# Attention products on four quarters of TensorE's array, roots with two dependent steps, and a reordered instruction schedule, in a convolution, attention and expert kernel

## What is computed

```python
# x: (32, 64, 32, 32)
x = x + conv(groupnorm(x))          # relu/sigmoid maps, their outer product (16x16), a 1x1 conv
t = tokens(x)                       # (32, 1024, 64)
# attention, on y = layernorm(t); H = 8 heads of D = 8
q, k, v = y @ Wq, y @ Wk, y @ Wv
Q, K = elu(q) + 1, elu(k) + 1
KV  = einsum('nshd,nshv->nhdv', K, v)
Z   = 1 / (einsum('nlhd,nhd->nlh', Q, K.sum(axis=1)) + eps)
msg = layernorm(einsum('nlhd,nhdv,nlh->nlhv', Q, KV, Z) @ Wm)
t = t + y + layernorm(relu(concat([y, msg]) @ W1) @ W2)
# experts, on z = layernorm(t)
t = t + sum_e cw[e] * (gelu(z @ W1[e] + b1[e]) @ W2[e] + b2[e])
```

## Time and profile before

| what | value |
|---|---|
| median of 3 runs | 1252.85 us (1252.80 to 1252.86) |
| profiled execution | 1252.97 us, its span 1251.2 us |
| PE busy | 1092.2 us, 87% of the span |
| DVE busy | 852.6 us, 68% |
| ACT busy | 699.9 us, 56% |
| POOL busy | 362.2 us, 29% |
| granted TensorE clock, mean | 0.978 of full speed |

### The profile page before, as it was taken

How to read it: one execution, slowest core, us unless ns; L and a number is a source line. 1 busy time by engine, 2 the same in 40 slices (tenths; PEclk the granted TensorE clock), 3 DMA queues, 4 the chain that set the end, 5 groups by cost and what they waited for, 6 DMA issues and landing times.

```text
span 1251.2 us, 14277 instructions
## 1 busy us (share of the span) xinstructions
PE 1092.2 (87%) x5238; PEld 501.4 (40%) x5238; DVE 852.6 (68%) x1751; ACT 699.9 (56%) x960; POOL 362.2 (29%) x276
## 2 busy tenths in 40 slices
PE   4776598979899799988989899997989979999897
PEld 2454244423544244442454334542444424534232
DVE  5656766697658876488585876669665887646433
ACT  3443365664665645755646656556466565566454
POOL 0100031233313423134313333124331333313466
PEclk8888699999999999999999999999999999999999
DMA  2110392008610094003920058100861019300570
GB/s 103 34 34 1 75 202 63 1 18 180 145 34 18 21 219 108 11 18 78 215 65 1 18 125 199 34 1 17 183 142 34 18 32 220 73 1 18 124 167 34
DMA packets 15797, 96.39 MB, mean 77 GB/s; under 512 B 2992, under 2 KB 5104, under 8 KB 11504
## 3 DMA queue, kind: packets, MB, share of 16 engines
q1 hardware_dynamic: 15728, 95.49, 32.7%
HBM read 77.66 MB, written 9.44 MB: 70 GB/s over the span
## 4 chain that ended last, share of the span: by engine, by line
PE 58%; DVE 25%; ACT 12%; issue 4%; DMA 1%; POOL 0%; DVEq 0%; POOLq 0%; SPq 0%; ACTq 0%
PE HP L647 10%; PE HP L662 9%; PE R L518 7%; PE R L586 5%; PE R L477 4%; PE R L488 4%; PE R L470 4%; DVE T L983 3%; PE R L532 3%; DVE TM L1100 2%; ACT H L788 2%; DVE SM L956 2%; PE R L561 2%; PE R L593 2%; PE R L662 2%
## 5 line engine op out<-in xcount | busy, mean ns | idle before, releaser
L828 POOL TENSOR_TENSOR XB<-TM,XB 128x512 f32<-128x512 f32 x256 | 324.8, 1289 | 825.2 <-DVE TM L1100 825.2
L788 ACT ACTIVATE H<-HP,W 128x1024 f32<-128x1024 f32 x224 | 237.7, 1114 | 98.9 <-PE HP L647 97.8
L647 PE MATMUL HP<-XF,W1E 64*128 64x512 f32 x1024 | 256.8, 620 | 25.5 <-DVE TM L1100 24.6
L662 PE MATMUL HP<-H,W 128*64 128x512 f32 x896 | 226.2, 611 | 29.1 <-ACT H L788 29.1
L1100 DVE SCALAR_TENSOR_TENSOR TM<-HP,B2S,CWB 128x512 f32<-128x512 f32 x224 | 159.4, 742 | 105.7 <-PE HP L662 102.1
L647 PEld LDWEIGHTS HP<-XF,W1E 64*128 64x128 f32 x1024 | 87.8, 186 | 150.4 <-DVE TM L1100 79.3
L956 DVE TENSOR_REDUCE SM<-T 128x8 f32<-128x512 f32 x128 | 86.3, 685 | 50.7 <-ACT T L725 49.3
L662 PEld LDWEIGHTS HP<-H,W 128*64 128x64 f32 x896 | 49.0, 135 | 176.9 <-ACT H L788 133.8
L725 ACT ACTIVATE T<-R 128x512 f32<-128x512 f32 x128 | 74.7, 597 | 79.1 <-PE R L518 77.7
L932 DVE SCALAR_TENSOR_TENSOR BIG<-R,T 128x512 f32<-128x512 f32 x128 | 79.8, 683 | 33.7 <-PE R L470 33.3
L488 PE MATMUL R<-W,T 128*128 128x128 f32 x512 | 78.0, 296 | 19.9 <-DVE T L975 19.0
(11 more groups left out here) (117 smaller groups left out, 1417.8 us busy)
## 6 DMA issues: line engine op xcount, KB each, us to landing
CWB<-gates_hbm SPq DMA_DIRECT2D x32, 1536.0 KB, 20.4
CWB<-gates_hbm SPq DMA_DIRECT2D x32, 512.0 KB, 6.7
X<-x SPq DMA_DIRECT2D x16, 512.0 KB, 6.5
BIG<-XN SPq DMA_DIRECT2D x32, 256.0 KB, 3.9
out<-XB SPq DMA_DIRECT2D x16, 512.0 KB, 2.7
W<-wpack SPq DMA_DIRECT2D x1, 1176.0 KB, 7.0
gates_hbm<-CWR SPq DMA_DIRECT2D x16, 64.0 KB, 1.6
W1E<-w1e SPq DMA_DIRECT2D x1, 512.0 KB, 8.4
```

Of the source, the lines that this page charges most:

```text
L647: last = mm(HP[u % BATCH][:, half(k)], W1E[img(k), e, :], XF[img(k), 1 - par, s, half(c)], start=True, stop=True)
L662: last = mm(sums_of(b, u)[img(k), :], w("w2e")[:, C * e:C * e + C], activated(b, u)[:, k, :], start=True, stop=True)
L788: f(activated(b, u).rearrange("p k t -> p (k t)"), HP[u % BATCH][:, :], ACT.Gelu, bias=col(B1E + e))\
L828: nc.gpsimd.tensor_tensor(acc, TM[:, u % BATCH, :], acc, ALU.add).then_inc(acc_done, 1)
```

## The change

It has three parts.

1. **Quarters.** `query` and `numerator` no longer use the block-diagonal 128x128 matrices but four products of 64x64 each, for a slot's two halves and two images. In the first half of the tokens image r goes from partitions `img(r)` to `img(r)`, in the second half it crosses to the other 64 partitions, so that the four products stand on four different quarters of the array; `numerator` crosses back. For the crossed half the key sums (`KS`), the values' matrix (`KVM`), the head mask (`HM2`) and `SPREAD` are needed in crossed form too. That adds a product with a swap matrix (`SWAP`) after each transpose of `kv_turn`, a second multiplication into `KS` on DVE, a copy of twice the width on ACT (`KXT`), a second product in `kv_values`, a multiplication of twice the width into `KVM`, and some small DMAs at the start. `query` now waits for both halves of `XB`, and `numerator` of slot 1 waits for L1006 before its first half, not its second.
2. **Roots.** `hz*y` is carried along as `hy`, so that a round has two steps that depend on each other, and an update of `hy` that is issued ahead of the update of `y` without a wait of its own.
3. **Schedule.** H and Y letters and some stages stand elsewhere in `SCHEDULE`. Entries that an engine has no part in leave its order alone. What differs on the engines: PE and ACT have one H ahead of `gates` and not behind it; `high_0`, `info_1` begin with slot 1; the order of `low_1` to `high_1` has its H after `low_1` and not between `info_1` and `low_1`; `first_unit` stands one batch earlier, so that 9 batches of a group run in its first turn and 7 in its second, where there were 8 and 8; an H that stood behind `hidden_1` stands ahead of `hidden_0`; `hidden_out` begins with slot 1 and its second slot comes ahead of the Y, and `tokens_3` begins with slot 0; `features_3.1` comes ahead of the Y.

The diff, cut to its core:

```diff
@@ SCHEDULE
-    ("channel_stats", ""), ("gates", "H"), ("gate_tokens", "Y"), ("gate_exp", ""), ("group_stats", "H"),
-    ("group_norm", "Y"), ("choose_1", ""), ("info_mask_0", "HY"), ("choose_2", "HY"), ("info_mask_1", "H"),
+    ("channel_stats", "H"), ("gates", ""), ("gate_tokens", "Y"), ("gate_exp", ""), ("group_stats", "H"),
+    ("group_norm", "Y"), ("choose_1", ""), ("info_mask_0", "HYH"), ("choose_2", "Y"), ("info_mask_1", "H"),
     ("gate_rows", "Y"), ("info_0.0", ""), ("info_0.1", "H"), ("low_0.0", ""), ("low_0.1", "Y"),
-    ("high_0.0", "H"), ("high_0.1", ""), ("info_1.0", "Y"), ("low_1.0", ""), ("info_1.1", "H"),
-    ("low_1.1", ""), ("high_1.0", ""), ("high_1.1", "Y"), ("first_unit", ""), ("conv_out.0", ""),
-    ("conv_out.1", ""), ("finish_1", ""), ("centre_1.0", ""), ("weights_1", ""), ("centre_1.1", ""),
-    ("rstd_1", "H"), ("norm_1.0", "Y"), ("features_1.0", ""), ("norm_1.1", "H"), ("features_1.1", ""),
+    ("high_0.1", ""), ("high_0.0", "H"), ("info_1.1", ""), ("info_1.0", "Y"), ("low_1.1", ""),
+    ("first_unit", ""), ("low_1.0", "H"), ("high_1.0", ""), ("high_1.1", "Y"), ("finish_1", ""),
+    ("conv_out.0", ""), ("conv_out.1", ""), ("centre_1.0", ""), ("centre_1.1", "H"), ("rstd_1", ""),
+    ("norm_1.0", ""), ("weights_1", "Y"), ("features_1.0", ""), ("norm_1.1", "H"), ("features_1.1", ""),
...
-    ("message.0", ""), ("message.1", ""), ("rstd_2", "H"), ("norm_2.0", ""), ("norm_2.1", "Y"),
-    ("features_2.0", ""), ("features_2.1", ""), ("hidden_0.0", ""), ("hidden_0.1", ""), ("hidden_1.0", ""),
-    ("hidden_1.1", "H"), ("hidden_out.0", "Y"), ("hidden_out.1", ""), ("tokens_3.1", ""),
-    ("tokens_3.0", "H"), ("rstd_3", "Y"), ("norm_3.0", "H"), ("norm_3.1", ""), ("features_3.0", "Y"),
-    ("features_3.1", ""), ("centre_4.0", ""), ("centre_4.1", ""), ("rstd_4", ""), ("finish_0", "H"),
-    ("norm_4.0", ""), ("norm_4.1", "Y"), ("features_4.0", ""), ("features_4.1", ""),
+    ("message.0", ""), ("message.1", ""), ("rstd_2", ""), ("norm_2.0", ""), ("norm_2.1", "HY"),
+    ("features_2.0", ""), ("features_2.1", "H"), ("hidden_0.0", ""), ("hidden_0.1", ""), ("hidden_1.0", ""),
+    ("hidden_1.1", ""), ("hidden_out.1", ""), ("hidden_out.0", "Y"), ("tokens_3.0", ""), ("tokens_3.1", ""),
+    ("rstd_3", "HY"), ("norm_3.0", ""), ("norm_3.1", "H"), ("features_3.0", ""), ("features_3.1", "Y"),
+    ("centre_4.0", ""), ("centre_4.1", "H"), ("rstd_4", ""), ("norm_4.0", ""), ("norm_4.1", "Y"),
+    ("features_4.0", ""), ("features_4.1", ""), ("finish_0", ""),
@@ PE
+        def crossed(c):
+            return [(r, r ^ c) for r in range(2)]
                 def query(slots):
-                    for s, c in pieces(slots):
-                        pe.wait_ge(xb_part[s], at(a + 1, c))
-                        mm(R[s][:, half(c)], w("wq"), XN[:, s, half(c)], start=True, stop=True).then_inc(qk_ps[s], 1)
+                    for s in slots:
+                        pe.wait_ge(xb_part[s], at(a + 1, LAST))
+                        for c in range(NCH):
+                            for r, k in crossed(c):
+                                last = mm(R[s][img(k), half(c)], w("wq", img(r))[:, img(r)], XN[img(r), s, half(c)],
+                                          start=True, stop=True)
+                            last.then_inc(qk_ps[s], 1)
                 def kv_turn(slots):
...
+                        nc.tensor.transpose(R[s][:, 0:P], KX[:, s, 0:P], w("ident")).then_inc(kvt_ps[s], 1)
+                        mm(R[s][:, CH:CH + 1], SWAP[:, :], KX[:, s, P:P + 1], start=True, stop=True).then_inc(ksum_ps[s], 1)
                 def kv_values(slots):
...
-                        mm(R[s][:, 0:P], KXT[:, s, :], w("wv"), start=True, stop=True).then_inc(kvm_ps[s], 1)
+                        for c in range(NCH):
+                            last = mm(R[s][:, P * c:P * c + P], KXT[:, s, C * c:C * c + P], w("wv"), start=True, stop=True)
+                        last.then_inc(kvm_ps[s], 1)
                 def numerator(slots):
-                    for s, c in pieces(slots):
-                        if c == 0:
-                            pe.wait_ge(kvm_done[s], a + 1)
-                        if (s, c) == (G - 1, LAST):
+                    for s in slots:
+                        pe.wait_ge(kvm_done[s], a + 1)
+                        if s == G - 1:
                             pe.wait_ge(den_eps, a + 1)
-                        mm(R[s][:, half(c)], KVM[:, s, :], Q[s][:, half(c)], start=True, stop=True).then_inc(num_ps[s], 1)
+                        for c in range(NCH):
+                            for r, k in crossed(c):
+                                last = mm(R[s][img(k), half(c)], KVM[img(r), s, c, img(k)], Q[s][img(r), half(c)],
+                                          start=True, stop=True)
+                            last.then_inc(num_ps[s], 1)
@@ ACT
                 def kv_turn(slots):
-                        f(KXT[:, s, :], R[s][:, 0:P], ACT.Copy).then_inc(kvt_done[s], 1)
+                        f(KXT[:, s, :].rearrange("p (n c) -> p n c", n=2), R[s][:, 0:P].unsqueeze(1).broadcast_to([P, 2, P]), ACT.Copy)\
+                            .then_inc(kvt_done[s], 1)
@@ DVE
                 def rsqrt(n, slots):
-                    hz, t, y = (SM[:, k, span, 0:n] for k in (1, 2, 3))
+                    hy, hz, t, y = (SM[:, k, span, 0:n] for k in range(4))
                     link(v.tensor_scalar(y.bitcast(I32), hz.bitcast(I32), -0.5, RSQRT_GUESS, ALU.mult, ALU.add))
-                    for _ in range(3):
-                        link(v.tensor_tensor(t, y, y, ALU.mult))
-                        link(v.tensor_tensor(t, t, hz, ALU.mult))
+                    link(v.tensor_tensor(hy, hz, y, ALU.mult))
+                    for last in (False, False, True):
+                        link(v.tensor_tensor(t, hy, y, ALU.mult))
+                        if not last:
+                            count(v.scalar_tensor_tensor(out=hy, in0=t, scalar=-1.5, in1=hy, op0=ALU.add, op1=ALU.mult))
                         link(v.scalar_tensor_tensor(out=y, in0=t, scalar=-1.5, in1=y, op0=ALU.add, op1=ALU.mult))
                 def key_value(slots):
-                        v.tensor_copy(KX[:, s, :], R[s][:, 0:P]).then_inc(kx_done[s], 1)
...
+                        v.tensor_copy(KX[:, s, :], R[s][:, 0:P + 1]).then_inc(kx_done[s], 1)
+                        key_sums(s, 0, R[s][:, P:P + 1])
+                def kv_turn(slots):
+                    for s in slots:
+                        dve.wait_ge(ksum_ps[s], a + 1)
+                        key_sums(s, 1, R[s][:, CH:CH + 1])
                 def kv_values(slots):
...
-                        v.tensor_tensor(KVM[:, s, :], R[s][:, 0:P], w("headmask"), ALU.mult).then_inc(kvm_done[s], 1)
+                        v.tensor_tensor(KVM[:, s, :, :].rearrange("p n c -> p (n c)"), R[s][:, 0:2 * P],
+                                        HM2[:, :], ALU.mult).then_inc(kvm_done[s], 1)
```

More of the change, by code:

```diff
@@ L380, in _ @@
                 sp.dma_start(GB[E * i:E * i + E, :], gb).then_inc(gb_in, 16)
+            masks = COLS["headmask"][0]
+            swaps = COLS["ident"][0]
+            sp.wait_ge(prep_done, 1)
+            for r, k in crossed(1):
+                sp.dma_start(HM2[img(r), P:2 * P], wpack[img(k), masks:masks + P]).then_inc(swap_in, 16)
+                sp.dma_start(SWAP[img(r), :], wpack[img(k), swaps:swaps + P]).then_inc(swap_in, 16)
             def parts(a, b, par):
```

47 lines of the change are left out of this document (30 added, 17 removed).

## The result

| | before | changed |
|---|---|---|
| median | 1252.86 us | 1232.61 us |
| runs | 1252.80 to 1254.65 (4) | 1229.98 to 1236.50 (4) |
| profiled execution, its span | 1252.97, 1251.2 us | 1232.37, 1230.6 us |
| ratio, 95% interval | | 0.9837, 0.9810 to 0.9865 |

The changed kernel is 1.6% faster.

The account below looks back on a forecast made before the run. PE was taken as close to the bound (132.15 of 146 us busy, 58% of the chain). Six steady turns at -3.0 us (-18), turn 0 -1.1, turn 1 +0.1, drain -4.75: -23.75 from 1252.97, so 1229 us; range 1221 to 1243.

Parts of the forecast that it names:

- Numerator: Numerator on the chain: one round per slot makes it 1.8 us shorter, 1.2 gained before reciprocal and combination limit it.
- Crossed copies: Extra swap products, wider copies and doubled products in kv_turn: cost of nothing to 0.9 us a turn, taken as 0.15.
- Roots: Each root from guess to scaling: 0.25 us saved, bounds nothing and 0.45; four in a turn, -1.0 us.
- (a): H ahead of gates, in the routing: with the group root's 0.25 us, 0.4 us sooner, bounds 0 and 0.6.
- (b): Outer product order: DVE's wait for PE at its end goes, -0.45 us a turn, bounds -0.9 and +0.5.
- (c): H ahead of hidden_0, in the hidden layer: about even, -0.1 us a turn, bounds -1 and +1.5.
- Turn 0: First turn: no Y between denominator and numerator, the reciprocal already bounds it, so only roots count: -1.1 us.
- rival of the clock: TensorE's clock falls in new idle places at query and numerator: 3 us a turn, 1250 us; chance 0.05.
- Turn 1: Second turn: gains 2.4 us, loses 2.5 (bounds 0 and 3.9) for one more batch; +0.1 us together.
- The drain: After the last turns: one batch less, 4.36 us each, nothing hiding them, so that time is saved.
- Two at a time: Rival: quarters run two at a time as before, numerator gains nothing, copies cost 0.15 us; 1237 us, chance 0.12.
- the shared bank: Rival: products writing one PSUM bank wait for each other, three rounds a slot instead of two; 1260 us, chance 0.10.

Follow-up runs that it names:

- diagonal: Changed kernel with nothing crossed: both token halves stay on the same two quarters, crossed copies still made but unused; 1237.33 us.
- quarters_alone: Kernel before with only the quarters and crossed copies, its own schedule and roots kept; 1252.85 us, ratio 0.9993.
- schedule_alone: Kernel before with only the new SCHEDULE; 1244.71 us, ratio 0.9931 to the kernel before.
- short_fill: Changed kernel plus unread products ahead of slot 1's query, ahead of attended (256 columns), and in turn 0 and turn 1's routing; 1224.71 us.
- unit_later: Changed kernel with only first_unit moved behind high_1.1, so 8 and 8 batches per group instead of 9 and 7; 1243.15 us.
- hidden_old: Changed kernel with the old hidden layer order: H behind hidden_1, Y between the slots of hidden_out, tokens_3 from slot 1; 1244.41 us.

## Why the prediction was right

1229 us was forecast, 1232.61 measured, inside the range and on the side given 0.86. The sum had -23.75 us; the profiled executions differ by 20.6 us. By its steps:

- **Numerator: right.** One round for a slot (1.95 us for two), then DVE's combination as the next limit, L1060 right behind it. The overlap is worth 1.16 us (`diagonal`) where 1.2 was the sum.
- **Query, nothing: right** for the time of the step, wrong for what its idle place does to the clock, though no fall behind it cost anything.
- **Crossed copies, 0.15 us: too low, within its bounds.** From rstd_1 to attended `quarters_alone` takes 0.88 us less than the kernel before (33.76 for 34.64), and the overlap gives 1.16: 0.28 us are the additions.
- **Roots, 0.25 us each: right**, and the group root arrives whole, where (a) had counted it as partly hidden: 1.24 us a turn alone.
- **Schedule (a), 0.4: too high**; the stage gained 0.27, no more than the root, and `schedule_alone` gained 0.03 there. **(b), 0.45: too low**, 0.73; the undoing gave 0.7. **(c), 0.1: right within its bounds**, 0.2 in the stage and 0.22 by the undoing. **(d), nothing: right.** From rstd_3 to rstd_4 0.21 us went where the root explains 0.25. The errors of (a), (b), (c) and the copies cancel, which is luck: 3.02 us a turn where 3.0 was said, six turns -18.1 us for -18.
- **Turn 0: the step that failed.** The sum had -1.1 us there. The channel statistics of turn 1 begin 4.3 us later than before and not 1.1 us sooner (124.23 for 119.94). The cause is the clock: `diagonal`, with the same work in turn 0 on two quarters, is there at 119.38 us, at 0.90 from the first numerator on where the changed kernel has 0.81, and with PE kept busy (`short_fill`, 1.00) it is 117.20 us. The prediction's term took every PE duration from rows at 1.00, although in the earlier trace rows the clock stood at 0.88, and its rival of the clock counted 3 us in each of seven turns and named no cost of turn 0.
- **Turn 1: right.** Its stage of the outer product grew by 2.6 us (14.04 for 11.47) for the extra batch counted at 2.5, and the turn, from channel statistics to channel statistics, shrank by 0.2 us where +0.1 was the sum. In `unit_later` the batch is 2.2 us of that stage, of which 0.7 is lost again ahead of attended.
- **The drain, one batch less: right**, 4.6 us for 4.36. Behind the last numerator 8.7 us went. The steps gave 6.8: 4.75 for the drain with (a), and of turn 7 the numerator's 1.2, three roots and (c). Of the 1.9 us above that, 1.6 is a fall of the clock that the kernel before had in its drain, with first layers of 3.55 us (1.99 is usual for these eight records), and the changed kernel not. No term of the sum had it; it made up for a part of turn 0 by luck. The timeline of before and the chain of the changed kernel, in the drain:

```profile
1164.73 3.55 PE L647 MATMUL HP<-XF,W1E 64*128 64x512 f32 x8 [2.68 <-DVE TM L1100]
```

```profile
1149.94 1.99 PE HP L676 x8
```

- **Rivals.** Two at a time and the shared bank: excluded, by L588 and by `diagonal`. A wait at hidden_out: not there, L622 follows without one. The clock: it exists, in both places named, so that the sign given for it (1.00 in all windows of turns 2 to 7) did not hold; but it costs 1.6 us in a turn in which it falls behind the numerator, nothing behind the query, and not 3 us in every turn. With 0.05 it was given too little, since the quarters alone gained 5.3 us by their quiet turns and 0.4 us in the median of ten runs.

The sum of the parts: -11.1 (roots), -0.4 (quarters), -8.5 (schedule) make -20.0 us, the whole -20.3. That the medians agree so well is in part chance, as each has other falls of the clock in it. The quiet turns are free of them: 1.24 + 0.88 + 0.93 = 3.05 us for 3.03, so that the three parts add up and none needs the others. Why the changed kernel seldom falls into the lower clock behind the numerator and three near variants of it often do is not settled; only that it hangs on PE's work in those two places, as added work there took it away in every profile. That the longest executions of the changed kernel (up to 1242.17 us) are such falls is argued from their mean clock, 0.964; none of them was profiled.

## What to carry to other kernels

Four products of 64x64 on four quarters cost one round, also where two share a bank on different partitions, and they pay only as far as the next limit behind them, here a reciprocal and a combination on DVE. After taking work from PE in front of an operand that comes no sooner, look at the granted clock behind that place, and at what stands there: a fall in front of work that waits anyway cost nothing here, one on the chain 1.6 us a turn, in some runs and not in others, and a spread of runs is the sign. Products that nobody reads, short enough to end before the operand comes, bought 8 us here, all of it in the first two turns, where PE waits for the other engines; in the steady turns they bought an even time, 0.6 us between five runs where it was 12. And read a stage in several turns before explaining it: 0.36 us of one turn were nothing of the change.

## What the runs showed of the hardware that was not expected

- The granted clock falls from 2.4 to 1.2 GHz (a reading of 0.72 or 0.60 is a stretch with both levels) where PE has hardly waited. In `hidden_old` it was 0.72 over 6 us behind the numerator (5.47 us for message products of 3.84); in the 7 us ahead of it PE was busy for 6.54 us at 1.00, with one wait of 0.46 us. The busy share does not announce it. In the kernel before, with a numerator of 3.63 us in the same place and no wait behind it, it was 1.00 in all steady turns.

```profile
786.00:793.00 7.00, 6.54 (x41) 2.03 (x34) 6.37 (x7) 2.06 (x4) 1.46 (x2) 1.00 0.31 72
```

- It repeats with the turn, and a change elsewhere in the turn can bring it on: the order of `hidden_old` differs from the changed kernel's only in a stretch that begins 15 us behind the numerator, and its falls stand 5 us behind the numerator of the next turns.
- With PE kept busy, turn 1 took 123.6 us, before it was 128.1 with a batch less in it.
- Two row tiles writing different partitions of one PSUM bank at once cost nothing (1.09 us for four products of 512 columns, against 1.07 for four on 32-column strips).
